# Down products on full 128-row chunks, peaks spread by transposition, a shorter warm-up and a new instruction order in a cross-attention and quantised FFN kernel

## The reference

```
x = x + xattn(layernorm(x), ctx):  q, k = ctx Wq' + bq, ctx Wk' + bk
                                   x_m = layernorm(x) @ softmax(q k')
x = x + ffn(layernorm(x)):
    quantise rows of x to fp8 (peak of a row = 448), the rows of w_gate and w_up likewise
    t = silu(g) * u                    (256*4 x 704)
    quantise rows of t and rows of w_down to fp8 alike
    y = t w_down', with the hidden columns in the order down_reorder_index
```

## Time and profile before

| | us |
|---|---|
| median of 3 runs (lowest, highest) | 79.10 (79.03, 79.25) |
| the profiled execution | 79.58 |
| its span, first to last instruction | 77.8 |
| PE busy | 69.9 (90%) |
| DVE, ACT, POOL busy | 61.1, 56.9, 49.0 |

### The profile page before, as it was taken

One profiled execution on the slowest core, in us unless ns is written; L12 is line 12 of the kernel. 1 busy time (PEld: TensorE's weight loads), 2 busy tenths in 40 slices (PEclk: granted clock), 3 DMA queues, 4 the chain that ended last, 5 costly groups with the idle time before them and its releaser, 6 DMA issues.

```text
span 77.8 us, 1587 instructions
## 1 busy us (share of the span) xinstructions
PE 69.9 (90%) x520; PEld 57.6 (74%) x520; DVE 61.1 (79%) x159; ACT 56.9 (73%) x118; POOL 49.0 (63%) x78
## 2 busy tenths in 40 slices
PE   4999999799959999999999999996989979998940
PEld 4999548589938988999887997984765746676710
DVE  1059899899995999988599999808999999992060
ACT  6106899997899889896899997996288371695400
POOL 5103135369649055987989887899998975853330
PEclk9999999999999999999999999999999999999999
DMA  0999899910000000000000011210240101042204
GB/s 13 272 414 418 258 366 412 409 53 8 0 4 4 0 0 0 0 0 8 0 0 0 34 38 34 67 24 1 85 118 0 67 0 56 11 135 71 70 6 135
DMA packets 4088, 6.98 MB, mean 90 GB/s; under 512 B 656, under 2 KB 2448, under 8 KB 4080
## 3 DMA queue, kind: packets, MB, share of 16 engines
q1 hardware_dynamic: 3888, 6.53, 23.5%
q0 software_dynamic: 192, 0.36, 1.4%
HBM read 5.48 MB, written 1.41 MB: 89 GB/s over the span
## 4 chain that ended last, share of the span: by engine, by line
PE 47%; POOL 22%; ACT 12%; issue 9%; DVE 7%; POOLq 0%; DVEq 0%; ACTq 0%
PE gate_ps L1258 9%; POOL act_g L402 9%; POOL wd_scatter L335 8%; PE tT_ps L1086 7%; PE gate_ps L1162 3%; PE up_ps L1137 3%; PE bank_s L1241 3%; PE tT_ps L1209 3%; PE tT_ps L1073 3%; ACT act_g L591 2%; DVE grid_t L769 2%; PE bank_s L1185 2%; DVE y_sb L892 2%; POOL qxT_bf L395 2%; ACT kT L495 2%
## 5 line engine op out<-in xcount | busy, mean ns | idle before, releaser
L402 POOL TENSOR_TENSOR act_g<-act_g,up_scale 128x704 f32<-128x704 f32 x8 | 13.6, 1695 | 1.1 <-ACT act_g L591 1.0
L1162 PE MATMUL gate_ps<-w_hi,qxT 128*128 128x352 f32 x32 | 11.0, 345 | 0.3 <-ACT act_g L591 0.3
L1209 PE MATMUL tT_ps<-ident,sum_t 128*128 128x128 f32 x48 | 10.4, 283 | 0.3 <-ACT tT L613 0.2
L383 POOL TENSOR_TENSOR sum_w<-sum_w,grid_w 128x256 f32<-128x256 f32 x6 | 4.1, 683 | 10.2 <-DVE sum_w L772 10.2
L1162 PE MATMUL gate_ps<-w_lo,qxT 128*128 128x352 f32 x32 | 10.2, 322 | 0.0
L414 POOL TENSOR_TENSOR x_sb<-y_sb,x 128x256 f32<-128x256 f32 x7 | 6.6, 945 | 5.6 <-DVE y_sb L892 5.6
L857 DVE TENSOR_TENSOR t_sb<-up_ps,act_g 128x704 f32<-128x704 f32 x8 | 7.1, 885 | 3.6 <-POOL act_g L402 2.2
L1212 PE MATMUL tT_ps<-negidentb,grid_t 128*128 128x128 bf16 x48 | 9.6, 219 | 0.0
L613 ACT ACTIVATE tT<-tT_ps 128x768 bf16<-128x768 f32 x7 | 5.7, 808 | 4.9 <-PE tT_ps L1212 4.7
L1086 PE MATMUL tT_ps<-attT,xT 128*128 128x256 f32 x32 | 7.6, 381 | 0.9 <-issue 0.9
L548 ACT ACTIVATE grid_w<-wup_sb,s_w 128x256 bf16<-128x256 f32 x12 | 5.2, 497 | 4.3 <-DVE s_w L808 4.3
(11 more groups left out here) (117 smaller groups left out, 203.6 us busy)
## 6 DMA issues: line engine op xcount, KB each, us to landing
wup_sb<-w_gate_up_dram SPq DMA_DIRECT2D x3, 512.0 KB, 4.8
x_sb<-x_dram SPq DMA_DIRECT2D x4, 256.0 KB, 8.0
xT<-x_t_dram SPq DMA_DIRECT2D x2, 512.0 KB, 9.6
out_dram<-x_sb SPq DMA_DIRECT2D x8, 128.0 KB, 1.7
wdn_sb<-w_down_dram SPq DMA_DIRECT2D x1, 704.0 KB, 6.6
head_sb<-head_dram SPq DMA_DIRECT2D x1, 416.0 KB, 5.4
wdnT<-wd_scatter SPq DMA_DIRECT2D x6, 64.0 KB, 1.9
ctx_sb<-ctx_t_dram SPq DMA_DIRECT2D x1, 256.0 KB, 6.8
```

The costliest lines, as they stand in the source:

```text
L402: nc.gpsimd.tensor_tensor(act_g[:, i % NT], act_g[:, i % NT], up_scale[:, :], ALU.mult)\
L1162: last = nc.tensor.matmul(ps[:, h, 0:IH], qxT[:, b, c, j * P:(j + 1) * P].bitcast(F32R), w[:, c, a, h * IH:(h + 1) * IH].bitcast(F32R), st ...
L1209: nc.tensor.matmul(to, sum_t[:, i % NT, of], ident[:, :], start=True, stop=False, is_transpose=True)
```

## The change

- `WARM_UP` is 15 instead of 24.
- `down` and `down_last` take all 128 rows of each chunk. For the last chunk wdnT holds zeros in its first 64 rows (a memset on POOL, in `constants`), and its read-back brings only the 64 fresh rows.
- `spread` and `spread_up` have `is_transpose=True`.
- ScalarE scales the tiles 0, 2, 4, 6 and 7 instead of 0, 3, 6 and 7; DVE sums 1, 3 and 5.
- All five queues have a new order: the loads; the down chunks' transpositions come ahead of gates(0); scatter(0) to (3) come ahead of scale_act(0), the fourth and fifth between the scalings; gates(7) comes behind down(0).

```diff
-WARM_UP = 24
-SCALED_BY_ACT = (0, 3, 6, 7)
-SUMMED = (1, 2, 4, 5)
+WARM_UP = 15
+SCALED_BY_ACT = (0, 2, 4, 6, 7)
+SUMMED = (1, 3, 5)
...
-                sp.dma_start(wdnT[:, k], wd_dram[chunk(k), :]).then_inc(wdnT_in, 16)
+                sp.dma_start(wdnT[P - fresh[k]:, k], wd_dram[P * k:P * k + fresh[k], :]).then_inc(wdnT_in, 16)
...
+                nc.gpsimd.memset(wdnT[0:P - fresh[KC - 1], KC - 1], 0.0)
...
-                    last = nc.tensor.matmul(y_ps[i], tT[P - fresh[k]:, i % 2, k], wdnT[P - fresh[k]:, k],
+                    last = nc.tensor.matmul(y_ps[i], tT[:, i % 2, k], wdnT[:, k],
...
-                                            peak_w[:, k, 1:2].to_broadcast([P, P]), ident[:, :], start=True, stop=True)
+                                            peak_w[:, k, 1:2].to_broadcast([P, P]), ident[:, :], start=True, stop=True,
+                                            is_transpose=True)
```

More of the change, by code:

```diff
@@ L904, in _ @@
             scales_up(0)
+            bn_stats1(0)
+            grids_up(0)
+            bn_aggr1(0)
+            sums_up(0)
             peak_of_up(1)
-            grids_up(0)
+            grids_up(1)
             reciprocal_up(1)
             scales_up(1)
-            grids_up(1)
-            sums_up(0)
-            grids_up(2)
-            peak_of_down()
-            sums_up(1)
-            bn_stats1(1)
-            bn_stats1(2)
-            score_max(0)
-            sums_up(2)
-            score_max(1)
@@ L919, in _ @@
-            reciprocal_of_z(0)
-            score_max(2)
-            bn_stats1(0)
-            reciprocal_of_z(1)
-            reciprocal_down()
+            sums_up(1)
+            score_max(0)
+            peak_of_down()
+            reciprocal_of_z(0)
+            score_max(1)
+            peak_of_up(2)
+            bn_stats1(1)
+            grids_up(2)
+            reciprocal_of_z(1)
+            bn_aggr1(1)
+            score_max(2)
+            reciprocal_up(2)
+            reciprocal_down()
@@ L941, in _ @@
-            grids_up(4)
-            split_up(1)
+            bn_aggr1(2)
+            score_max(3)
+            bn_stats2(0)
+            grid_down(0)
+            split_up(0)
+            bn_aggr2(0)
+            grids_up(3)
+            reciprocal_of_z(3)
+            bn_aggr1(3)
+            sums_up(3)
+            sum_down(0)
             residual(1)
             peak_of_x(0)
-            sums_up(4)
+            grid_down(1)
             reciprocal_x(0)
+            split_up(1)
             grids_up(5)
@@ L948, in _ @@
             scales_x(0)
+            grids_up(4)
+            sum_down(1)
+            sums_up(4)
+            split_up(2)
             bn_stats2(1)
-            split_up(2)
+            grids_x(0)
             bn_aggr2(1)
             sums_up(5)
-            grids_x(0)
-            bn_aggr1(2)
-            bn_aggr1(3)
             split_up(3)
+            residual(2)
             peak_of_x(1)
-            sum_down(0)
+            split_up(4)
             reciprocal_x(1)
             scales_x(1)
-            split_up(4)
+            bn_stats2(2)
@@ L962, in _ @@
             split_up(5)
-            residual(2)
+            bn_aggr2(2)
+            residual(3)
             grids_x(1)
-            grid_down(1)
-            sum_down(1)
-            bn_stats2(2)
-            bn_aggr2(2)
-            hidden(0)
-            peak_of_t(0)
             peak_of_x(2)
-            reciprocal_t(0)
             reciprocal_x(2)
             scales_x(2)
+            bn_stats2(3)
+            bn_aggr2(3)
+            hidden(0)
+            grids_x(2)
+            peak_of_t(0)
@@ L1249, in down_last @@
                 for k in (range(0, HALF_CHUNKS) if h == 0 else range(HALF_CHUNKS, KC)):
-                    last = nc.tensor.matmul(y_ps[LAST], tT[P - fresh[k]:, LAST % 2, k], wdnT[P - fresh[k]:, k],
+                    last = nc.tensor.matmul(y_ps[LAST], tT[:, LAST % 2, k], wdnT[:, k],
                                             start=(k == 0), stop=(k == KC - 1))
@@ L1267, in _ @@
             scores(0)
+            turn_up(0)
+            scores(1)
             spread()
-            scores(1)
+            turn_att(0)
             scores(2)
-            turn_up(0)
-            turn_att(0)
             turn_up(1)
-            scores(3)
             attend(0)
             turn_att(1)
+            scores(3)
+            turn_att(2)
+            attend(1)
+            spread_up(0)
             turn_up(2)
-            attend(1)
-            turn_att(2)
+            spread_up(1)
+            turn_att(3)
+            turn_down(0, 0)
+            attend(2)
+            turn_down(0, 1)
             turn_up(3)
-            spread_up(0)
-            attend(2)
-            spread_up(1)
+            turn_down(1, 0)
             turn_up(4)
+            turn_down(1, 1)
             turn_x(0)
             turn_up(5)
-            turn_att(3)
-            turn_down(0, 0)
+            attend(3)
             gates(0)
-            turn_down(0, 1)
             turn_x(1)
@@ L1293, in _ @@
             ups(0)
-            turn_down(1, 0)
             gates(2)
-            turn_down(1, 1)
             ups(1)
-            attend(3)
+            turn_x(2)
+            gates(3)
             ups(2)
-            gates(3)
-            turn_x(2)
             turn_t(0)
@@ L1304, in _ @@
             ups(3)
+            turn_x(3)
+            gates(5)
+            ups(4)
             turn_t(1)
-            gates(5)
-            turn_x(3)
-            turn_t(2)
-            ups(4)
             gates(6)
             ups(5)
+            turn_t(2)
+            down(0)
             gates(7)
-            down(0)
-            ups(6)
             down(1)
             turn_t(3)
-            ups(7)
+            ups(6)
             down(2)
@@ L1320, in _ @@
             down(3)
+            ups(7)
             turn_t(5)
```

229 lines of the change are left out of this document (108 added, 121 removed).

## The result

| | before | after |
|---|---|---|
| median (lowest, highest), 4 runs each, us | 79.17 (79.03, 79.27) | 83.75 (82.61, 83.98) |
| ratio to before, 95% interval | | 1.049 (1.039 to 1.060) |
| the profiled execution, its span | 79.58, 77.8 | 83.98, 82.2 |

The change makes the kernel slower by 4.9%; the forecast was 78.2, faster.

A forecast was written before the change was run, and what follows sets the result against it. PE was busiest (90%), but stretches had different limits; the read-back was to hold down(0) at 58.5. With 15.25 behind it, PE ends at 73.75 instead of 74.66: 0.9 off the 79.10 median gives 78.2, range 76.4 to 79.9.

The forecast's parts named there:

- The inputs are there: Between the scatters: silu(0) done about 37.5 and silu(3) about 46, before POOL needs them at 39.4 and 47.4.
- The sum for POOL itself: POOL from scatter(0) at 32.7 to the last scatter's end at 50.9: 18.2 us of scatters, scalings and smaller passes.
- The start: Warm-up of 15 products, head loaded second: projections start at 6.2 instead of 8.14, -1.9, clock risen within the 15.
- Up to the scatters: Walk of the new queues: attend(1) at 21.1, gates(0) at 35.0, scatter(0) at 32.7 instead of 42.5.
- rival 3: Scatters ahead of scalings starve TensorE: slower, decided from scatter(0) at 33.6; 80.2 with DVE 2 late; 18%.
- From the last scatter to down(0): Read-back between last scatter's end and first down product: 7.57 us that no engine can shorten, down(0) at 58.5.
- Held by the read-back: Rival 1, the forecast itself: down(0) waits for the read-back, -0.9, own range 77.3 to 78.9; 42%.
- From down(0) on: PE's tail from the first down product: 15.25 us instead of 16.2, bounds 14.0 and 16.5.
- Full rows: Down products on 128 rows: 0.2 to 0.26 saved for each of 8, -1.6 to -2.1 of PE work.
- The spreads: Peaks spread by transposition: eight products lose one record each, -0.95 of PE work, bounds 0 and -0.95.
- The fifth scaled tile: One tile more scaled by ScalarE: six more records on PE, +0.34; DVE loses one pass of 0.94.
- rival 4: Clock falls back or rises later, after the shorter warm-up and PE's idling around 13 us: 80 to 81; 7%.

The follow-up runs named there:

- e3: The changed kernel with POOL's scalings multiplying by a constant in place of up_scale (the short scalings, 0.77 each); 78.28 us, ratio 0.984.
- e1: The changed kernel with each of POOL's scalings replaced by two memsets that read nothing (the memsets); 79.80 us, ratio 0.994.
- g1: The kernel before with 15 warming products, the head loaded second, full-row down products and transposed spreads, without the new order; 79.32 us, ratio 0.990.
- h1: The changed kernel with gates(3) ahead of turn_x(2) on PE and silu(3) ahead of abs_t(0) on ACT; 85.03 us, ratio 1.074.
- b1: The kernel before with only full-row down products and transposed spreads; 80.28 us, ratio 1.001.
- c4: The kernel before with only 15 warming products and the head loaded second; 79.28 us, ratio 0.995.
- c1: The changed kernel with grids_x(2) ahead of hidden(0) on DVE and scatter(4) between scale_act(1) and scale_act(2) on POOL; 84.57 us, ratio 1.057.
- the quarters: The changed kernel with each of POOL's scalings cut into four passes over 176 columns; 85.09 us, ratio 1.064.
- a1: The changed kernel with grids_x(2) moved ahead of hidden(0) in DVE's queue; 84.76 us, ratio 1.052.
- e2: The kernel before with each of POOL's scalings replaced by two memsets; 80.18 us, ratio 1.010.
- e4: The kernel before with POOL's scalings multiplying by a constant in place of up_scale; 79.15 us, ratio 0.989.
- g5: The kernel before with 15 warming products, head loaded second, full-row downs, transposed spreads and scalings by a constant; 78.34 us, ratio 0.980.

## Why the prediction was wrong

**The step that failed** is "The inputs are there", and with it the walk of the middle. I gave DVE's passes the durations of rows in which they ran free and laid POOL's scalings beside them at no cost. They aren't free of each other. I had silu(3) at about 46 and POOL at its scaling at 47.4; silu(3) started at 51.41 and POOL's scaling at 52.34, after a wait of 3.59. The sum for POOL itself was right: from scatter(0) to the end of the last are 22.47 us (34.13 to 56.6), which is my 18.2, this wait, and 0.7 by which the last scatter was longer. So the last scatter ended at 56.6 and not at 50.9, and down(0) was at 62.33 and not at 58.5. The kernel before has it in its trace (three grids of t with 0.82 to 1.44, 0.39 elsewhere), and I read over that. The new order puts two scalings in a row under DVE's busiest stretch: 3.46 at `grids_x(2)` alone. What the change would bring without the hold at scalings of full length, no run shows. With the clock up, the memsets, which leave 2.96 of excess, take 79.20 to 79.86; the short scalings, 0.9 shorter each, take 76.98.

**The start.** PE was to be free at 6.2; the projections start at 7.25. Timeline of PE, the kernel after:

```profile
1.06 6.35 PE L1260 MATMUL gate_ps<-warm_w 128*128 128x128 f32 x30 [1.06 <-DVE warm_w L903]
```

The 30 records are all there; the clock rose at 6.83 in this trace, at 4.46 in that of before, and until then a record takes about twice as long. In e3 it rose at 4.68 and the projections started at 6.23, as counted. The count was right; that the rise leaves the later ones of the 15 at the upper level was an assumption: over the traces it lies between 4.06 and 7.28 us.

**Up to the scatters.** attend(1) at 21.4 (I said 21.1), gates(0) at 35.7 (35.0), the last subtraction over at 32.68 (32.7): right. Scatter(0) came at 34.13: the last copy of wdT ended at 33.28 (I had 32.4), and the scatter started 0.85 behind it, for which I had nothing. By rival 3 this delay of 1.4 is past its mark (33.6) and puts down(0) near 59.9. That part was real, PE's 1.47 behind `scale_act(0)` among it; the way on to 62.33 it doesn't explain, as e1 and e3, with scatter(0) at 33.78 and 35.19, have down(0) at 59.05 and 58.00.

**From the last scatter to down(0)** I took 7.57 as fixed. It is 5.7 in the kernel after (56.6 to 62.33), 7.3 in g1, 8.4 in h1. Before, PE came free within 0.3 of the data, so the interval was set twice over, and I put it all down to the read-back. "Held by the read-back" was wrong for the forecast, too: PE goes from turn_t(2) straight into down(0), 0.16 after the last load has landed (62.17).

**From down(0) on** I said 15.25; it took 16.57. e3 (58.00 to 73.07) and e1 (59.05 to 74.13) took 15.1: the sum was near, and what these two lack is the sum_t held for 1.36 and the wait of 0.87 behind it.

**The parts.** Full rows: six products took 0.65 where they took 0.84, and the wait ahead of the last weight load is gone, as said; the term had 0.26. The spreads show 8 records where they showed 16, as counted. Whether it pays depends on what else holds: 0 in b1, 1.0% together with the edits of c4 (0.5% by themselves) in g1. The fifth scaled tile wasn't run alone; its cost is inside the difference between g1 and the kernel after.

**Rivals.** The clock of rival 4 was real and small, and at another place (47.79, not around 13): every timed run of the kernel after has 0.973 to 0.979, worth about 1.2 by the runs of e1. It fell behind the waits of 1.47 and 2.87. That POOL and DVE exclude each other stood in none of the five, although the Trainium skill states it in the section named above; it belonged there, with the three long grids of t in the trace of before as evidence.

**What stays open.** How the 4.66 of idle time divide over the single holds and the late `scale_act(0)` isn't settled: each variant that moved one made another, and several had a low clock elsewhere. Nor is what lets DVE in: behind two-input scalings in a row it isn't let in, with 0.2 passes between them neither (c1; at the quarters it got in late), while a cast or a power behind a scaling let it in (57.62 in the kernel after, which ends at 59.21 with POOL's scaling at 59.01). Nor is the part of the scatters: in a1, c1, e2, e4 and g5 a held pass began under the end of one, while in the kernel before `grid_x` at 50.16, under the last scatter (49.87 to 50.88), took its 0.30.

## What to carry to other kernels

When two queues are reordered, lay the passes of VectorE and GpSimd over each other by their times and price each overlap at the rest of GpSimd's run, through passes that follow it without a gap. Before a walk, look for instructions of one kind with very different durations: a pass of two columns with 2.4 us is a wait in disguise, and the page's list of waits doesn't show it. And an interval between two events is a constant only if nothing else arrives at the same moment.
